# GpSimd's scatters in one row behind head 126, in an attention and mixture-of-experts kernel

## The reference

```python
x = x + _layernorm(attention(_layernorm(x)))      # q, k normed and rotated, causal softmax, w_o
xf = _layernorm(x)
logits = xf @ gate_w.T                            # 8 experts
weights, indices = top_k(softmax(logits), 2)      # two experts per token
h = silu(xf @ w_gate[e]) * (xf @ w_up[e])
out = sum over e of combine[t, e] * (h @ w_down[e])
out = out + sigmoid(xf @ shgate_w) * shared_expert(xf)
x = x + _layernorm(out)
```

## Time and profile before

| | |
|---|---|
| median of 3 runs | 688.54 us (687.67 to 688.94) |
| profiled execution | 686.81 us, span 684.9 us |
| TensorE busy (matmul) | 634.6 us, 93% |
| VectorE busy | 568.9 us, 83% |
| ScalarE busy | 564.8 us, 82% |
| GpSimd busy | 555.8 us, 81% |
| indirect scatters to `xs` (L2106) | 32, first at 486.7 us, last at 551.5 us |
| granted TensorE clock | 0.977 on average |

### The profile page before, as it was taken

One profiled execution on the slowest core, in us unless ns is written; L12 is line 12 of the kernel. 1 busy time (PEld: TensorE's weight loads), 2 busy tenths in 40 slices (PEclk: granted clock), 3 DMA queues, 4 the chain that ended last, 5 costly groups with the idle time before them and its releaser, 6 DMA issues.

```text
span 684.9 us, 15537 instructions
## 1 busy us (share of the span) xinstructions
PE 634.6 (93%) x4430; PEld 583.0 (85%) x4430; DVE 568.9 (83%) x1925; ACT 564.8 (82%) x2175; POOL 555.8 (81%) x590
## 2 busy tenths in 40 slices
PE   3669999999999999999999999999789989999993
PEld 2457899999999999999999998899678889999981
DVE  6899999998989889888888889999979855555466
ACT  5678999999989999998999999899888535666634
POOL 6799889999999999999999998989867324666554
PEclk9697999999999999999999999999999999999997
DMA  8001023999440000000000000000436033443263
GB/s 345 4 1 32 13 91 104 334 335 283 3 46 1 2 1 2 1 1 2 1 2 1 2 1 2 1 1 25 145 112 224 33 89 109 125 126 118 78 246 123
DMA packets 50978, 54.20 MB, mean 79 GB/s; under 512 B 19824, under 2 KB 42608, under 8 KB 50768
## 3 DMA queue, kind: packets, MB, share of 16 engines
q1 hardware_dynamic: 47488, 43.84, 21.8%
q0 software_dynamic: 3408, 9.38, 3.7%
HBM read 23.76 MB, written 29.51 MB: 78 GB/s over the span
## 4 chain that ended last, share of the span: by engine, by line
POOL 60%; PE 21%; ACT 8%; issue 5%; DVE 3%; DMA 1%; another core or an unknown queue 0%; SPq 0%; ACTq 0%; POOLq 0%; DVEq 0%
POOL ropes L2013 13%; POOL ropes L2023 13%; POOL ropes L2016 11%; POOL rs L2001 10%; POOL hrow L2037 3%; POOL osb L2044 2%; POOL rs L1999 2%; PE pQ L458 2%; PE pQ L460 2%; PE pQ L459 2%; ACT ropes L973 2%; POOL lr L2001 2%; ACT P L988 1%; PE pO L458 1%; PE pA L731 1%
## 5 line engine op out<-in xcount | busy, mean ns | idle before, releaser
L458 PE MATMUL pQ<-W 128*128 128x512 f32 (+2 forms) x334 | 119.4, 357 | 10.2 <-DVE W L1382 5.3
L988 ACT ACTIVATE P<-P,nmx 128x128 f32<-128x128 f32 (+1 forms) x256 | 120.6, 505 | 0.0
L459 PE MATMUL pQ<-W 128*128 128x512 f32 (+2 forms) x334 | 114.5, 343 | 0.0
L460 PE MATMUL pQ<-W 128*128 128x512 f32 (+2 forms) x334 | 114.3, 342 | 0.0
L996 ACT ACTIVATE P<-P,rinv 128x128 f32<-128x128 f32 (+1 forms) x256 | 107.6, 496 | 1.7 <-DVE rinv L1455 1.6
L2013 POOL TENSOR_TENSOR ropes<-ropes 128x640 f32<-128x640 f32 x63 | 98.8, 1569 | 7.3 <-DVE ropes L1428 7.3
L2023 POOL TENSOR_TENSOR ropes<-ropes 128x640 f32<-128x640 f32 x63 | 99.4, 1578 | 4.9
L973 ACT ACTIVATE ropes<-pQ 128x128 f32<-128x128 f32 x320 | 90.3, 315 | 14.6 <-POOL ropes L2023 12.3
L458 PE MATMUL pO<-W 128*128 128x256 f32 (+1 forms) x323 | 94.6, 293 | 5.5 <-DVE W L1464 2.9
L1459 DVE TENSOR_TENSOR W<-pP,W 128x384 fp32r<-128x384 f32 x128 | 70.3, 549 | 28.0 <-ACT W L1001 27.7
L459 PE MATMUL pO<-W 128*128 128x256 f32 (+1 forms) x323 | 91.5, 283 | 0.0
(11 more groups left out here) (268 smaller groups left out, 2225.8 us busy)
## 6 DMA issues: line engine op xcount, KB each, us to landing
xs<-stage SPq DMA_DIRECT2D x1, 17550.0 KB, 58.4
stage<-xs SPq DMA_DIRECT2D x39, 130.0 KB
ropes<-in_ew SPq DMA_DIRECT2D x8, 608.0 KB
stage<-in_wqkv SPq DMA_DIRECT2D x3, 768.0 KB, 8.7
stage<-ys SPq DMA_DIRECT2D x4, 512.0 KB, 6.3
ropes<-ys SPq DMA_DIRECT2D x4, 512.0 KB, 7.4
out<-X SPq DMA_DIRECT2D x7, 256.0 KB, 2.0
X<-in_wo SPq DMA_DIRECT2D x1, 1536.0 KB, 13.3
```

The costliest lines, as they stand in the source:

```text
L458: e.matmul(out, lh, rh, start=start, stop=False, skip_group_check=True)
L459: e.matmul(out, lh, rl, start=False, stop=False, skip_group_check=True)
L460: return e.matmul(out, ll, rh, start=False, stop=stop, skip_group_check=True)
L988: a = e.activation(P[:, z, span(t)], P[:, z, span(t)], ACT.Exp, bias=nmx[:, z, t:t + 1], scale=-1.0, accum_out=sums[:, z, t:t + 1])
```

## The change

On GpSimd alone. From tile 3 on, the single waits for `s_PT` go and one wait for `s_PT` >= 126 stands ahead of tile 3; the waits for `s_uact` >= 2, 3 and 4 go. `out_root(7)` moves from behind both scatters of tile 11 to between the two of tile 8. `ln2_root(7)` moves from behind both scatters of tile 12 to between the two of tile 10. The number of scatters and roots and what they compute stay. No other engine's list changes.

```diff
             sw_lo(2)
-            e.wait_ge(s_PT, NHEAD - 6)
+            e.wait_ge(s_PT, NHEAD - 2)
             scatter(0, 3, 0)
             scatter(0, 3, 1)
-            e.wait_ge(s_PT, NHEAD - 5)
             scatter(0, 4, 0)
             scatter(0, 4, 1)
-            e.wait_ge(s_PT, NHEAD - 4)
             scatter(0, 5, 0)
             scatter(0, 5, 1)
-            e.wait_ge(s_PT, NHEAD - 3)
             scatter(0, 6, 0)
             scatter(0, 6, 1)
-            e.wait_ge(s_PT, NHEAD - 2)
             scatter(0, 7, 0)
             scatter(0, 7, 1)
-            e.wait_ge(s_PT, NHEAD - 1)
             scatter(0, 8, 0)
+            out_root(7)
             scatter(0, 8, 1)
-            e.wait_ge(s_PT, NHEAD)
             scatter(0, 9, 0)
             scatter(0, 9, 1)
-            e.wait_ge(s_uact, 2)
             scatter(1, 10, 0)
+            ln2_root(7)
             scatter(1, 10, 1)
-            e.wait_ge(s_uact, 3)
             scatter(1, 11, 0)
             scatter(1, 11, 1)
-            out_root(7)
-            e.wait_ge(s_uact, 4)
             scatter(1, 12, 0)
             scatter(1, 12, 1)
-            ln2_root(7)
             scatter(1, 13, 0)
             scatter(1, 13, 1)
```

## The result

The changed kernel took 696.62 us (median of 4 runs, 695.34 to 699.15) against 688.74 us for the kernel before in the same measurement (4 runs): ratio 1.0141, 95% interval 1.0111 to 1.0171. No ratio in this document includes one execution of e12 that took 795.86 us at a granted clock of 0.753. The forecast was 689.3 us with a range to 690.3 us; the time lies 6.3 us outside. The instruction lists of TensorE, VectorE and ScalarE are the same as before; only GpSimd's differs.

The account below looks back on a forecast made before the run. TensorE was taken as busiest, GpSimd's order touching critical work only at `ln2_root(7)`. The removed waits, later row and transfers cost nothing; the late root adds 0.8 us to the 688.54 us median: 689.3 us, range 687.1 to 690.3 us.

Parts of the forecast that it names:

- Part 1: GpSimd's waits ahead of the scatters from tile 3 on: removal costs nothing; the row starts at 513.74 us.
- Rival (d): Stretch before 513.85 us: if scatters cause ScalarE's "remote" waits, up to 1.89 us return, 686.6 to 687.5 us; chance 0.20.
- Parts 2 and 3: GpSimd's row and `out_root(7)`: `ln2_root(7)` starts at 535.6 us, its power is held by VectorE's L1503, ScalarE 0.83 us later.
- rival (c): `ln2_root(7)` held from its first instruction: 1.35 us, or up to 2.0 us, 689.9 to 690.5 us; chance 0.22.
- (a): Likeliest: the held power of `ln2_root(7)` loses 0.8 us, or 1.07 us: 689.3 to 689.6 us; chance 0.35.
- Part 4: Seven scatters behind `ln2_root(7)` end at 547.0 us, 1.5 us remain free before the last slots: cost nothing.
- Part 5: Expert weight loads overlapping the row: late landing bounded at 0.8 us, a wait of 0 taken at `ew_hi(4)`.
- Theory R: Formed after the result: the places of the two roots or the order of the later scatters cost the time.

Follow-up runs that it names:

- e12: The changed kernel with the old single waits back and the two roots at their new places, on chip 12: 682.03 us, ratio 1.0008 to the kernel before.
- e11: The changed kernel again, unchanged, as the control on chip 12: 682.88 us, ratio 1.0013 to the kernel before.
- e5: The changed kernel again, unchanged, on chip 1: 698.76 us, ratio 1.0149 to the kernel before.
- e6: The kernel before again, unchanged, for a profile on chip 1: 687.07 us, ratio 0.9995 to the kernel before.

## Why the prediction was wrong

**Where the time went.** Three executions at the same points of the program, in us (the first two on chips with late signals, the third on chip 12):

```
                                    before    after   after, chip 12
wait for head 126 ends (GpSimd)     513.74   509.97   510.55
ln2_apply(7) starts (ScalarE)       537.21   540.75   535.09
last slots' scatters (GpSimd)       547.75   555.54   545.64
first gathered tile (TensorE L703)  558.73   567.39   555.77
span                                684.9    693.8    681.8
```

The changed kernel wins 3.8 us up to the row, loses 7.3 us in it (from 3.8 ahead to 3.5 behind), 4.3 us more up to the last slots (the second row, seven scatters from 540.89 to 549.55 us), and 0.9 us up to the first gathered tile, with TensorE at the lower clock level. After that the gap stays, 8.9 us at the end.

**Part 1 is the step that failed**: "no engine waited for a scatter there, so I cost the removal at nothing". True of the scatters' results, wrong of their company. By the traces of the two occasions near 688 us, the waits that went away were pauses in which TensorE's signals came through: late by up to 3.5 us before, by up to 9.4 us with the row of eleven, where 7.3 us were lost, and by up to 4.3 us with the row of seven, where 4.3 us more were lost. The start of the row, 513.74 us, was wrong for the same reason: that time held 3.8 us that the kernel before had lost beside its own six scatters.

**Rival (d)** saw the right place and had the sign wrong. Its first half came true to the row: ScalarE's waits near 510 us went, worth 3.8 us where I allowed 1.89 us (a third one, 0.38 us ahead of 510.17 us, I had left out). But I wrote "I see no tie to GpSimd". Had I followed the unplaced "remote" to its partner, the six scatters that stand beside it, the next question would have been what a row of eleven does. A price of even 0.5 us for each of five more scatters would have outweighed all other terms. No rival had this cause on the side of slower.

**Parts 2 and 3** did not come about in the measured execution. VectorE's statistics of block 7 ended at 538.53 us (538.28 + 0.25), `ln2_root(7)` started 0.16 us later, as before, and its power took 0.72 us; only L2060 was held (0.66 us), as before. The delays ahead had made the statistics of block 7 later than the row: its fourth scatter behind `out_root(7)` ended at 538.40 us, before them. On chip 12, where nothing covers them, they can be read. GpSimd and VectorE of e11:

```profile
510.55 0.98 POOL L2106 DMA_INDIRECT xs<-stage,slots  x1 [11.36 <-DVE W L1459]
...
524.03 0.96 POOL L2106 DMA_INDIRECT xs<-stage,slots  x1 [0.30 <-issue]
525.06 0.33 POOL L1999 TENSOR_SCALAR lr<-mv 128x2 f32<-128x2 f32 x1
525.47 1.64 POOL L2001 TENSOR_TENSOR lr<-lr,half 128x2 f32<-128x2 f32 x1
527.30 1.80 POOL L2106 DMA_INDIRECT xs<-stage,slots  x1 [0.20 <-issue]
...
533.07 0.66 POOL L2057 TENSOR_SCALAR nb<-mv 128x2 f32<-128x2 f32 x1
533.79 0.19 POOL L1999 TENSOR_SCALAR lr<-mv 128x2 f32<-128x2 f32 x1
534.07 0.72 POOL L2001 TENSOR_TENSOR lr<-lr,half 128x2 f32<-128x2 f32 x1
...
545.64 0.96 POOL L2106 DMA_INDIRECT xs<-stage,slots  x1 [1.28 <-DVE slots L1663]
```

```profile
525.36 1.16 DVE L1503 TENSOR_TENSOR W<-ropes,W 128x960 fp32r<-128x960 f32 x1
...
531.24 0.25 DVE L1529 BATCH_NORM_AGGREGATE mv<-st 128x2 f32<-128x6 f32 x2
...
532.47 1.18 DVE L1503 TENSOR_TENSOR W<-ropes,W 128x960 fp32r<-128x960 f32 x1
```

The power of `out_root(7)` (525.47 us) met the L1503 of 525.36 to 526.52 us and ended at 527.11 us, 0.59 us after it; the prediction had 0.60 us. The scatter of 527.30 us took 1.80 us beside the next L1503. Then `ln2_root(7)` came to stand behind the row, its first instruction held (0.66 us instead of 0.23 us), its power free. That is rival (c), by the way it named: `out_root(7)` held first. Its price shows against e12, the same chip with the old waits:

```profile
524.13 0.20 POOL L1999 TENSOR_SCALAR lr<-mv 128x2 f32<-128x2 f32 x1 [8.35 <-DVE mv L1478]
...
531.65 0.23 POOL L2057 TENSOR_SCALAR nb<-mv 128x2 f32<-128x2 f32 x1 [1.12 <-DVE mv L1529]
...
544.26 0.96 POOL L2106 DMA_INDIRECT xs<-stage,slots  x1 [1.73 <-DVE slots L1663]
```

```profile
533.71 1.09 ACT L1036 ACTIVATE stage<-X,nb,lr 128x256 f32<-128x256 f32 x2 [2.21 <-POOL nb L2060]
```

`ln2_root(7)` is 1.42 us later (533.07 against 531.65), ScalarE 1.38 us (535.09 against 533.71), the last slots 1.38 us (545.64 against 544.26); rival (c) had 1.35 us. The spans differ by 1.7 us, the medians by 0.85 us, and neither ratio is certain to differ from 1. So the sum of the prediction, +0.8 us, was near what the medians give on a chip without late signals (+1.1 us on chip 12, 682.88 against 681.81 us; +2.2 us on chip 13, both within the noise), partly by luck: the route was (c) and not the (a) that the sum was made of. It said nothing of the other kind.

The rule of the Trainium skill ("SBUF — State Buffer", section Who interferes with whom), by which a VectorE `tensor_tensor` should not stall descriptor generation, would have let the row escape. The scatter of 527.30 us disagrees with it once more: 1.80 us against 0.96 us.

**Part 4** held on chip 12: the seven scatters ended at 544.35 us (543.39 + 0.96), 1.28 us before the slots. In the measured execution their own time cost nothing either (5.99 us of idle time before the slots), but beside them `s_logits` came 2.79 us late, and the slots hang on it. **Part 5** held: the copy of weights at 516.07 us (L1029) has no recorded wait.

**What is shown and what is open.** Shown: on the two occasions with the kernel before near 688 us the change costs 1.4% and 1.5%, on chips 12 and 13 the ratios, 1.0013 and 1.0020, can't be told from 1; where it costs most, TensorE's signals arrive up to 9.4 us after its matmuls, in time with rows of scatters, and in the 16 traces from the other chips none of them recorded between 498 and 575 us is more than 0.02 us late. Theory R is excluded for the first loss by the order of time alone: the waits ahead of 520.06 and 521.42 us lie ahead of both roots (531.36 and 538.69 us), and up to there the kernels differ only in the scatters' waits. Not shown by an experiment: that the old waits or an even pitch cure it on such a chip, for none of those kernels fell on one; the kernel before, with rows of six, two, eight, two, two and four, is the nearest case. Its rows say that the number alone doesn't decide: beside the six, 1.38 us apart on average, signals were up to 3.5 us late, beside the eight from 518.41 us, 1.48 us apart, at most 1.2 us, and four in the changed kernel (532.56 to 538.40 us), 1.63 us apart, left them on time, though these are also fewer. That fits the pitch as the cause; no run shows it. Open is also why chips differ, and whether the number of scatters without a pause, their descriptors or their bytes hold the signals up. So is one rival that no run tests, the recording itself. Every execution of the experiments has a recorded span and clock, none was timed without, and the four traces with late signals (before, after, e5, e6) hold 1662 to 1730 records of landed DMAs where all others hold 2527 or more. For the changed kernel it is 1730 and 1662 against 2532 and 2534, with the same 15537 instructions and 50992 DMA packets; up to 450 us the counts agree in all traces. Something in how such updates are passed on or recorded differs there, for DMAs too. The kernel before is slower there as well, 684.9 us of span against 680.1 us for e12; 3.2 us of these 4.8 are lost by head 126 (513.74 against 510.55 us in e11, whose list pauses until then), beside its six scatters; the rest is not traced.

## What to carry to other kernels

A wait that nothing needs can still be a pause that something else needs, as on the two occasions here: before long rows of GpSimd's indirect DMAs are formed, look whether the other engines' waits, above all those that the profile gives as "remote", stand beside the short rows that are there already. A wait that can't be explained is not evidence of nothing; follow it to what runs at the same time, and give the case in which it grows a price and a chance. And measure the changed kernel on more than one chip before a cause is sought in the code: the kernel before, measured beside each experiment, was what showed that two kinds of chips were being mixed.

No version beat the kernel before in a way that repeats: the best, the old waits with the roots moved forward (e1's kernel), had ratios of 1.0010, 0.9976, 1.0008, 1.0007, 1.0010 and 0.9997, of which only 0.9976 on chip 13 lies clear of 1.

## What was not expected of the hardware

- TensorE's completion signals can arrive 2.8 to 9.4 us after the matmul, in bursts (0.07 us apart), while GpSimd issues indirect scatters of 128 rows every 1.27 us, and VectorE's and ScalarE's arrive 0.01 us after their ends beside them. It was so in the first measurement and on chip 1. On chips 12 and 13 the same list had none of it, with as busy a DMA (0.94 against 0.97), nor had a row of 18 scatters on chip 3; on chips 8 and 10 the changed kernel did not run.
- The traces with late signals also hold fewer records of landed DMAs (1662 to 1730 against 2527 and more).
- After such a pause (TensorE at 0.00 of 2 us) the granted clock is at 0.50, the 1.2 GHz level, for some 7 us (0.54, 0.50 and 0.76 in the windows from 520 to 528 us), though the pause came only from late signals.
- The same program took times 1% apart on two chips: 680.9 us on chip 3 and 687.6 us on chip 1 for the kernel before.
